# The second mixture of eight begins on ten tiles ahead of the last batch's routing

## Time and profile before

| what | value |
|---|---|
| median of 3 runs | 1555.32 us (1548.15 to 1560.02) |
| the profiled execution | 1545.64 us |
| its span, first to last instruction | 1543.8 us |
| mean granted TensorE clock | 0.911 of 2.4 GHz |
| busy: PE, DVE, ACT, POOL | 1208.7, 833.3, 729.7, 727.5 us |
| shares of the chain that ended last | PE 53%, DVE 14%, issue 11%, DMA 7%, POOL 6%, ACT 3%, SPq 3% |

### The profile page before, as it was taken

One profiled execution on the slowest core, in us unless ns is written; L12 is line 12 of the kernel. 1 busy time (PEld: TensorE's weight loads), 2 busy tenths in 40 slices (PEclk: granted clock), 3 DMA queues, 4 the chain that ended last, 5 costly groups with the idle time before them and its releaser, 6 DMA issues.

```text
span 1543.8 us, 23348 instructions
## 1 busy us (share of the span) xinstructions
PE 1208.7 (78%) x7329; PEld 798.8 (52%) x7329; DVE 833.3 (54%) x2723; ACT 729.7 (47%) x1494; POOL 727.5 (47%) x968
## 2 busy tenths in 40 slices
PE   3219989689999999999629978725999777469994
PEld 2219878322232322222219967624889656448884
DVE  6542146688898999888222445461223677512124
ACT  3214444167777767677414543422444466324431
POOL 3564755222233535524544555563554357735543
PEclk9999999799999999999759989857999987679997
DMA  9156777744454344241056865433558321135576
GB/s 280 44 148 191 216 217 227 205 133 132 108 152 145 90 141 123 67 143 37 15 142 190 248 194 166 132 117 108 168 169 256 105 75 70 40 108 177 161 237 202
DMA packets 164073, 226.83 MB, mean 147 GB/s; under 512 B 20656, under 2 KB 123440, under 8 KB 163952
## 3 DMA queue, kind: packets, MB, share of 16 engines
q1 hardware_dynamic: 119152, 174.05, 39.1%
q0 software_dynamic: 18304, 37.65, 7.2%
q10 hardware_dynamic: 26496, 13.64, 3.1%
HBM read 152.81 MB, written 72.20 MB: 146 GB/s over the span
## 4 chain that ended last, share of the span: by engine, by line
PE 53%; DVE 14%; issue 11%; DMA 7%; POOL 6%; ACT 3%; SPq 3%; another core or an unknown queue 2%; ACTq 0%; POOLq 0%; DVEq 0%
PE PS L1344 16%; PE PS L1334 16%; PE PS L1443 5%; PE PS L1466 5%; DVE arena L2126 5%; POOL dispatched L706 3%; PE PS L1324 2%; PE PS L1451 2%; DMA arena<-experts 2%; PE PS L1429 1%; POOL dispatched L896 1%; DMA YC<-expert_out 1%; ACT arena L1064 1%; DVE BST L1721 1%
## 5 line engine op out<-in xcount | busy, mean ns | idle before, releaser
L734 POOL DMA_INDIRECT expert_out<-arena x316 | 304.4, 963 | 350.7 <-issue 242.3
L970 ACT ACTIVATE arena<-PS,arena 128x256 f32<-128x256 f32 (+1 forms) x568 | 266.7, 498 | 405.0 <-PE PS L1334 356.7
L1064 ACT ACTIVATE arena<-PS 128x512 f32<-128x512 f32 x512 | 286.2, 596 | 130.1 <-PE PS L1443 121.4
L1334 PE MATMUL PS<-arena 128*128 128x256 f32 (+1 forms) x1136 | 313.4, 418 | 20.9 <-issue 11.2
L1344 PEld LDWEIGHTS PS<-arena 128*128 128x128 f32 x2528 | 311.7, 196 | 25.8 <-issue 10.6
L1344 PE MATMUL PS<-arena 128*128 128x128 f32 x2528 | 315.7, 280 | 8.7 <-DVE arena L1998 7.3
L2126 DVE TENSOR_REDUCE arena<-PS 128x2 f32<-128x1024 f32 x256 | 302.6, 1218 | 21.7 <-PE PS L1453 19.9
L1998 DVE TENSOR_TENSOR arena<-PS,arena 128x256 f32<-128x256 f32 (+1 forms) x142 | 64.5, 454 | 408.1 <-PE PS L1344 312.7
L1334 PEld LDWEIGHTS PS<-arena 128*128 128x128 f32 x1136 | 210.0, 196 | 75.3 <-issue 18.7
L706 POOL DMA_INDIRECT dispatched<-arena x192 | 185.3, 965 | 102.7 <-issue 59.9
L1443 PE MATMUL PS<-arena 96*128 96x512 bf16 x512 | 173.2, 392 | 12.7 <-ACT arena L1064 7.1
(11 more groups left out here) (258 smaller groups left out, 1231.5 us busy)
## 6 DMA issues: line engine op xcount, KB each, us to landing
arena<-experts SPq DMA_DIRECT2D x142, 578.0 KB
qk_products<-arena SPq DMA_DIRECT2D x48, 384.0 KB
arena<-qk_products SPq DMA_DIRECT2D x64, 288.0 KB
arena<-dispatched SPq DMA_DIRECT2D x110, 129.0 KB
dispatched<-FILL SPq DMA_DIRECT2D x32, 322.5 KB
YC<-expert_out ACTq DMA_DIRECT2D x40, 256.0 KB
arena<-qk_products SPq DMA_DIRECT2D x64, 128.0 KB
arena<-dispatched SPq DMA_DIRECT2D x32, 193.5 KB
```

The lines of the kernel that those rows point to most:

```text
L734: pool.indirect_dma_start(YK, bass.IndirectOffsetOnAxis(ap=ID[:, s:s + 1], axis=0), YS[:, s, :], None).then_inc(s_yo[r], 16)
L970: act.activation(HT[:, tau % PAIR, q, 0:S * P], hidden_chunk(S, q), func, bias=WE[:, r, 2 * DFF + q:2 * DFF + q + 1]).then_inc(s_g, 1)
L1064: act.activation(PT[:, G % 2, j, k, :], bank(4 + k % 2), ACT.Exp, scale=float(1.0 / np.sqrt(HD))).then_inc(s_exp, 1)
L1334: pe.matmul(hidden_chunk(size(f, tau), q), WE[:, r, q * P:q * P + P], XPT[:, tau % PAIR, 0:N], start=True, stop=True).then_inc(s_h, 1)
```

## The change

`early_tiles` gives BEGUN = 10 for the second mixture of eight. Its first table is made in group 31 (`count_first` on TensorE in step 1, `first_table` on VectorE in step 2), from batches 0 to 4. SyncE loads rows and experts of ten tiles as soon as that table is there, group 30 is weighed, and batches 0 to 4 have been sent. The steps behind group 32's place are replaced by a list written out on TensorE, VectorE and ScalarE, in which turn, hidden, outputs, gelus, copies and biases of tiles 0 to 9 alternate with the last batch's projection, residual, statistics, deviation, rows, logits, choice and ranks. All counts and the main table come behind tile 4's outputs. The deviation of the last batch is worked out by `inverse_deviation` on VectorE (12 steps) in place of a square root on ScalarE. GpSimd's list is as before: the last batches' sends, then scatters from tile 0. ScalarE's four tails stand behind tile 6's gelus; SyncE's four tails, and its wait for all sends, stand behind the loads of expert 9. The tile loop starts at tile 10. As ten tiles hold rows of the first five batches only, `start_of` for the carried batches is at least BEGUN + E0 + 3 + 2b: the first tile steps go from 15, 19, 23, 27, 31, 35, 40, 42 to 21, 23, 25, 27, 31, 35, 40, 42.

```diff
+BEGUN = 10
         def early_tiles(L):
-            return SOON if L == 0 else 0
+            return SOON if L == 0 else BEGUN if under_attention(L) else 0
...
-            return max(tiles_to(b) + (4 if carries(L) else 6), early_tiles(L) + E0 + 4 + 2 * b if early_tiles(L) else 0)
+            if carries(L):
+                return max(tiles_to(b) + 4, early_tiles(L) + E0 + 3 + 2 * b)
+            return max(tiles_to(b) + 6, early_tiles(L) + E0 + 4 + 2 * b)
...
                 if soon:
                     sp.wait_ge(s_soon, first_kind(f) + 1)
+                if under_attention(L):
+                    sp.wait_ge(s_av, GROUPS - 1)
+                    for u in range(2):
+                        sp.wait_ge(s_batch[u], 16 * 2 * GT * ((KNOWN + 1 - u) // 2))
+                    for tau in range(RING):
+                        rows_in(tau)
+                        expert_in(tau)
+                    for tau in range(RING, XRING):
+                        rows_in(tau)
+                    early_loads()
...
+                elif r == KNOWN - 1:
+                    more.then_inc(s_known, 1)
+                    pool.wait_ge(s_known, first_kind(f) + 1)
...
+                ranks(NG - 2, 2)
+                out_rows(r)
+                for tau in range(3):
+                    tile_gelus(f, tau)
+                batch_rows(r)
+                last_rows()
+                tile_gelus(f, 3)
+                ranks(r)
+                for tau in range(4, 7):
+                    tile_gelus(f, tau)
+                clear_tails(f)
+                for tau in range(7, BEGUN):
+                    tile_gelus(f, tau)
...
+                r = NG - 1
+                route_ranks(NG - 2, 2)
+                pe.wait_ge(*read)
+                turn_values(GROUPS - 1)
+                tile_turn(fr, 0)
+                pe.wait_ge(s_td, GROUPS)
+                turn_out(r)
+                tile_turn(fr, 1)
...
+                tile_hidden(fr, 0)
+                project(r)
+                tile_hidden(fr, 1)
+                tile_outputs(fr, 0)
+                tile_turn(fr, 2)
+                tile_hidden(fr, 2)
+                tile_outputs(fr, 1)
+                pe.wait_ge(s_od, NG)
+                turn_rows(r)
+                tile_turn(fr, 3)
+                tile_hidden(fr, 3)
+                route_logits(r)
+                tile_outputs(fr, 2)
+                tile_turn(fr, 4)
+                pe.wait_ge(s_lgc, NG * fr + NG)
+                route_ranks(r)
+                tile_outputs(fr, 3)
+                tile_hidden(fr, 4)
+                tile_turn(fr, 5)
+                tile_hidden(fr, 5)
+                tile_outputs(fr, 4)
+                count_all(fr, bank(5, 0, NG * E0))
+                for tau in range(6, BEGUN):
+                    tile_turn(fr, tau)
+                    tile_hidden(fr, tau)
+                    tile_outputs(fr, tau - 1)
+                tile_outputs(fr, BEGUN - 1)
...
+                normalised(GROUPS - 1)
+                rows_turned(f, 0)
+                rows_turned(f, 1)
+                residual(NG - 1)
+                rows_turned(f, 2)
+                last_rows()
+                outputs_out(f, 0)
+                rows_turned(f, 3)
+                outputs_out(f, 1)
+                for part in range(2):
+                    choose(NG - 1, part)
+                outputs_out(f, 2)
+                rows_turned(f, 4)
+                outputs_out(f, 3)
+                rows_turned(f, 5)
+                outputs_out(f, 4)
+                rows_turned(f, 6)
+                main_table(f, bank(5, 0, NG * E0), True)
+                outputs_out(f, 5)
+                for tau in range(7, BEGUN):
+                    rows_turned(f, tau)
+                    outputs_out(f, tau - 1)
+                outputs_out(f, BEGUN - 1)
```

More of the change, by code:

```diff
@@ L319, in build @@
         s_av0 = sem("av_bank_cleared")
-        s_v7, s_d7 = sem("last_variance_ready"), sem("last_deviation_ready")
+        s_d7 = sem("last_deviation_ready")
         s_d0 = sem("first_deviation_ready")
@@ L616, in moe @@
                         expert_in(tau)
-                for tau in range(RING, soon):
-                    sp.wait_ge(s_yc, T0 + tau - (RING - 1))
-                    if tau + XRING - RING < soon:
-                        rows_in(tau + XRING - RING)
-                    expert_in(tau)
+                if not under_attention(L):
+                    early_loads()
                 if S == S0:
@@ L964, in gelus @@
                 def gelus(tau):
-                    r, S = tau % RING, size(f, tau)
-                    for q in range(FC):
-                        act.wait_ge(s_h, tau * FC + (T0 * FC + q + 1))
-                        if q == 0 and tau >= PAIR:
-                            act.wait_ge(s_y, T0 + tau - (PAIR - 1))
-                        act.activation(HT[:, tau % PAIR, q, 0:S * P], hidden_chunk(S, q),
-                                       func, bias=WE[:, r, 2 * DFF + q:2 * DFF + q + 1]).then_inc(s_g, 1)
+                    tile_gelus(f, tau)
                 def carried_rows(b):
@@ L994, in first_middle @@
                     act.activation(QP[:, 1, w, :], QR[:, w, :], ACT.Copy).then_inc(s_mid0, 1)
-                for c in range(0, last_step(L) + 1 if carries(L) else tiles):
+                for c in range(begin(L), last_step(L) + 1 if carries(L) else tiles):
                     if c < tiles:
@@ L1097, in step @@
                         batch_rows(NG - 2, 0)
-                    if j == 0 and G == GROUPS + 1:
-                        ranks(NG - 2, 2)
-                    if j == 2 and G == GROUPS + 2:
-                        last_deviation()
                     if j == 3 and g == 2 and batch(b + 2):
@@ L1387, in first_values @@
                     mm.then_inc(s_proj, 1)
-                turn(0)
-                turn(1)
-                hidden(0)
-                for c in range(1, last_step(L) + 1 if carries(L) else tiles + 1):
+                turn(begin(L))
+                turn(begin(L) + 1)
+                hidden(begin(L))
+                for c in range(begin(L) + 1, last_step(L) + 1 if carries(L) else tiles + 1):
                     if c + 1 < tiles:
@@ L1876, in rows_and_experts, with first_table @@
                 dve.tensor_tensor(rows, SC[:, 2:3], cst("tilerow"), ALU.add).then_inc(done, 1)
-            def first_table(f, counts):
+            def first_table(f, counts, early):
                 n = KNOWN * E0
@@ L1954, in moe @@
                     route(L)
-                if E == E0:
+                if E == E0 and not under_attention(L):
                     main_table(f, bank(6, 0, NG * E), early_tiles(L) > 0)
@@ L2035, in moe @@
                 fronts = range(FRONTS if E == E1 else 0)
-                tile_in(0)
-                tile_in(1)
-                for c in range(1, last_step(L) + 1 if carries(L) else tiles + 1):
+                tile_in(begin(L))
+                tile_in(begin(L) + 1)
+                for c in range(begin(L) + 1, last_step(L) + 1 if carries(L) else tiles + 1):
                     if c + 1 < tiles:
@@ L2220, in step @@
                         choose(b - 2, 0)
+                    if j == 2 and G == GROUPS - 1:
+                        first_table(f, bank(3, 0, KNOWN * E0), BEGUN)
+                f = ffn_of(L + 1)
                 dve.wait_ge(s_yc, TILES0[ffn_of(L)])
```

178 lines of the change are left out of this document (101 added, 77 removed).

## The result

The changed kernel took 1569.79 us (median of 6 runs, 1566.2 to 1571.37) against 1557.68 us of the kernel before (6 runs): a ratio of 1.0079, interval 1.0051 to 1.0107, 12 us slower where 19 us faster was forecast. Its profiled execution took 1570.25 us (span 1568.4, clock 0.915) against 1545.64. On two further chips the same pair gave 1.0084 and 0.9941; why they differ in sign is half of what follows. The execution profiled before, at 1545.64 us, is quicker than each of the six timed ones (1548.15 to 1562.89), so the 24.6 us between these two traces overstate the 12 us of the medians.

The account below looks back on a forecast made before the run. The prediction took GpSimd's list of sends to set the stage's end, with routing and loads filling the hole before. Its terms, -19.6 - 7.8 + 8.5 = -18.9 us from 1555.3, gave 1536.4, say 1536.5 us; range 1524 to 1552.

Parts of the forecast that it names:

- Part 1: Hole before the second mixture: ten tiles run there, tile 10 starts at 825 instead of 844.57 us, -19.6 us.
- the sum: Ten early tiles: hidden(0) at 765.5 us plus tiles, batch 7's work and stalls puts tile 9's end at 815.8 us.
- the seam: Between tiles 9 and 10: SyncE's tails, row loads and expert 10 end at 823 us, plus 2 us for the clock.
- the sum of stalls: Early tiles: VectorE's last-batch work delays outputs of tiles 0 and 2, 3 us each; table 1 us, tail issues 2 us.
- Part 2: Tiles 10 to 38: carried batches begin later and closer, 147.6 instead of 155.4 us, -8 us, bounds -12 and +6.
- two more each: Part 2's slow bound: two more us in each of three crowded pairs of tiles, +6 us.
- Rival (a): Tiles after 20: GpSimd bounds the stage, sends cost tiles nothing; Part 2 is 0, -11 us, 1544; with (b) 0.25.
- Part 3: Behind the last tile: twelve more sends, 15.0 us, first fill a 6.7 us wait; +8.5 us, bounds +7 and +15.
- (b): Between tiles 9 and 10: a longer seam, to 833 us, 8 us more lost, -11 us, 1544; with Rival (a) 0.25.
- (d): Early tiles: at 1.2 GHz throughout, ten cost 36 us more, tile 10 at 861, +17 us, 1572; chance 0.08.

Follow-up runs that it names:

- e6: Changed kernel with carried batches begun at the old tile steps (15, 19, 23, 27, 31, 35): 1442.74 us, 0.9859 on chip 2; 1549.06 us, 1.0012 on chip 3.
- e4: Changed kernel with four chained memsets behind every second send after the last tile, up to batch 6's own: 1567.82 us, 1.0055.
- e2: Kernel before with only the changed kernel's later starts of carried batches, no early tile: 1564.99 us, 1.0048.
- The probe: Separate program, not the kernel: chained tiny steps on VectorE and ScalarE while GpSimd issues indirect sends, with or without pauses; no kernel time.
- g1: The probe with 48 sends and seven kinds of pause (none included), on chip 2: no slow step; no kernel time.
- g2: e6 with four chained memsets behind each tile's two scatters and two sends, and every 4th send of the tail: 1464.87 us, 1.0008, chip 2.
- e7: Changed kernel with four early tiles instead of ten, carried batches at the old starts: 1455.49 us, 0.9947.
- e8: Changed kernel with batch 5's eight sends held until tile 1's hidden layer is done: 1465.32 us, 1.0013.
- g4: e6 with batch 5's eight sends held until tile 1's hidden layer is done: 1445.99 us, 0.9890.
- e1: The probe's first run: 200 steps per engine in six phases, 32 sends with or without pauses and expert loads: 18 VectorE steps over 1 us.

## Why the prediction was wrong

| on top of the kernel before | chips with slow steps | without |
|---|---|---|
| later starts alone | 1.0048 | not run |
| ten early tiles alone | 1.0012 | 0.9859 |
| both, the change | 1.0079, 1.0084 | 0.9941 |

**Part 1 (tile 10 at 825, -19.6 us) failed on the chip that was forecast for, and was rightly sized elsewhere.** Where no slow steps are, the order ran as laid out: 21.7 us up to tile 10, and -20.6 us for the kernel (e6). In e6 tile 9's bias is out 54.5 us after the last weighing (772.75 - 718.22), where the sum had 55.1 (815.8 - 760.7), and the seam took 5.7 us, where it had 9.2. On the first chip tile 10 began at 850.82, 6.3 us later than before (5.9 later on chip 3), behind pauses of which VectorE's alone are 31.4 us. The step that failed is the sum of stalls, "3 us each": it took every wait to end when its operand is there. What the runs showed in its place are VectorE's starts up to 12.9 us after the operand, within runs of indirect transfers, on the chips that have slow steps. The pauses were to be seen in the trace of before (VectorE idle 7.61 us to 951.86 and 7.84 us to 1003.15, "remote", both within runs of sends), and I read the slow tiles there as crowded work. The move set more such runs, 18 transfers from 802.7 us, beside the tiles.

**Part 2 (-8 us) failed twice.** Tiles 10 to 38 took 151.7 us, 3.7 less than before and not 7.8 less. Two steps with two batches in them take 9.3 us, where two more each had been the bound. More important, it is no gain at all: the prediction itself says that GpSimd's list of sends sets the end of this stage, and a tile that comes earlier moves the end only if the first send does. Rival (a) priced part 2 at 0, and that price was right. Its reason, that sends cost the tiles nothing, is right on chip 2 (4.58 us a tile from 20 to 38 in e6) and wrong where there are slow steps (6.37).

**Part 3 (+8.5 us) was mis-sized, and is the step that failed on all chips.** The twelve sends were to fill the wait for batch 6's places first. They are 15.2 us, and the wait grew from 6.7 to 12.51 us (5.31 to 8.47 on chip 3), since slow steps hold the very chain that it waits for: with e4's pauses it is gone. On chips without slow steps hardly any wait is there to fill (1.77 us in e6). Parts 2 and 3 together were +0.5; they measured +7 (e2), +12.2 (chip 3) and +12.0 (chip 4 against chip 2).

**Rivals.** (b), a longer seam, fell: it is 3.3 us in the changed kernel (tile 9's bias 847.52 to tile 10's hidden layer 850.82) and 5.7 in e6. (d), the clock, was the rival for slower and not the cause: 0.79 was granted over the hole, and e6 gave its 20 us at 0.95 granted from 720 to 780 us, though one tile's outputs ran at half clock (3.56 us instead of 1.95). The kernel became slower not by the clock but by a term that was missing from all cases: engines held by sends.

**The Trainium skill** says in SBUF — State Buffer, section SBUF: two separate sides, that on the engine side only the port pair shared by VectorE and GpSimd causes contention, and that ScalarE never waits on anyone. The probe on chips 1 and 3 neither breaks that rule nor is explained by it: a copy of ScalarE keeps its 0.31 us and a step of VectorE its 0.16 beside sends, and what grows is the time between two of them, on ScalarE as well.

**Still open.** What the slow steps are: sends back to back cause them and pauses remove them, but no run shows what holds the engines. Why the first pause (8.57 us before 771.55) begins when only three sends have run, beside tile loads, while in the probe the first slow step comes 12.8 us into a run: its test was on chip 2 alone. Whether a sparser pause would do on a chip with slow steps: g1 and g2 ran where there is nothing to cure. And what in those chips is different, and whether the slow steps are all of the 94 us between them.

**The best version** is e6, where batches are gathered at the old starts: 0.9859 on chip 2, and 1.0012 on chip 3, which is level with the kernel before and ahead of the changed one. It relies on these data: its starts and its waits for outputs are below the bound of the kernel's rule, so with other routing a batch could be gathered before its last tile is out. It measures what the early tiles are worth and is no kernel to keep as it stands. e7 keeps the rule, 0.9947 on chip 2.

## What to carry to other kernels

When one engine's list sets the end of a stage, count from its first item on: a later start is paid, less the items that it leaves out of the stretch (29.6 us later and twelve transfers fewer ended 17.2 us later, e8 against g4), and neither faster work upstream nor a wait seen in the list pays it back. Before work is moved beside a long run of indirect sends, look in the trace for waits that nothing on the chip explains; 0.6 us of other GpSimd work behind every second send cured them in e4's tail, and such a pause cost 0.6 to 1.1 us of GpSimd's time, in full where GpSimd was full. Time a change on more than one chip before believing a per cent.

## What the hardware showed that was not expected

- On two of four chips a back-to-back run of indirect sends (1.26 us each) raises dependent steps on VectorE and ScalarE from 0.20 and 0.34 to up to 1.40 us. On VectorE it begins 11 to 13 us after the run's start, on ScalarE later (18 us in e1), and ends some 4 us behind the last send. On the two others VectorE's steps stay at or under 0.27 us beside 48 sends in a row (chip 2) and 32 (chip 4).
- The same kernel takes 1547 to 1558 us on the former and 1463 to 1466 on the latter, 6% apart, although the sends' period is the same.
- Four chained memsets of 8 columns, 0.6 us, behind every second send brought VectorE's deviation steps back to 0.20 us (e4); 1.8 us did so in the probe.
- Such a pause can cost more than the 0.6 us of its memsets: 1.1 us between the tiles of g2, where the next transfer starts 0.80 us behind them, and 0.6 in e4.
